# First gather stage of a two-layer graph kernel: attention products moved to a PSUM bank of their own, denominators copied out by ScalarE

## Chip, cores and metric

One core of one Trainium2 chip. The metric is the device time of one execution in microseconds (us), the median of repeated runs. Engines in profile rows: PE (TensorE matmul), PEld (its weight load), DVE (VectorE), ACT (ScalarE), POOL (GpSimd), SP (SyncE, which issues DMAs).

## What is computed

A two-layer graph network on 6,250 nodes of 256 features and 100,000 edges sorted by target. The stage of the change computes, of layer 0, the neighbour sums with the first matmul of the graph block, and the linear attention:

```python
agg = segment_sum(xn[src], dst)                 # 100,000 rows gathered
h1 = (agg + xn) @ W1                            # 1024 columns, batch statistics
q, k = elu(q) + 1, elu(k) + 1                   # of rmsnorm(xn) @ w_qkv
z = 1 / (q . sum(k) + 1e-6)                     # "denominators", per head
h = xn + ((q * z) @ kv) @ w_out + b_out         # "product" is (q * z) @ mix
x0 = x + h + rmsnorm(h)
```

`mix` is kv times w_out, 256x256, made once. Beside this the stage computes the edge network of layer 1 for the first edges (10 to 64 features, Silu, 64 to 1), which the change only has as a neighbour.

## The kernel before, in words

The stage is the phase "g1". Each engine has a queue written out in advance: `timeline` (called at lines 861, 880, 958, 1199, 1397) goes over steps 0 to 737 and, for each work item, emits its parts at fixed numbers of steps ("lags") behind the item's own step. The order on every engine is thus fixed by tables; semaphores (`Steps.wait`) order the engines among themselves. In the lists (`dens`, `zs`, `outs`, `hsum`, ...) `X.wait(e, i, "name")` waits for that part of item i.

- **Gathers** (line 876, POOL): one indirect DMA of 128 rows a step, steps 0 to 701, into 12 pairs of buffers (`got`). Gather 24 later waits for the sums of the pair (`summed`).
- **Sums** (`sums`, line 1261, PE): 8 matmuls per pair of gathers with a one-hot matrix (made by DVE, line 598), ten steps after the pair. DVE adds the result to a ring (`accumulate`, lines 1063 and 1072). The results lie in two PSUM banks; in the pairs of groups behind the edge network (`AFTER`) in four, 0, 1, 2 and 7 (`bank_of`).
- **Up-projection** (`turn_h` 1380, `form_h` 1084, `project_up` 1393, `copy_up` 944, `stats` 1189): 25 batches of 250 nodes. For each PE turns the own rows, DVE adds the ring, PE does 4 x 8 matmuls, ACT copies, DVE takes statistics. Batches come 14 to 22 steps apart, the last one at step 716.
- **Attention** (`ATT`): 50 tiles of 125 nodes, one every 7 steps, the first at step 333. SP loads queries, rows and x (`load_att`, lag 0, behind the last addition of tile i-4). PE: denominators (`denominators`, 1328, lag 8). DVE: `divide` (lag 10) copies them out of PSUM with 1e-6 added (1136), inverts (1138), multiplies with the queries (1140). PE: product (`product`, 1335, lag 13). DVE: `add_h` (1150, lag 15). Then ACT square, root, gate (915, 923, 929), and DVE `finish` (1159, 1161, lag 29). Lag 15 of tile i-1 and lag 8 of tile i are the same step.
- **Edge network** (`EDGE`, steps 391 to 451, its parts up to step 464): hidden layer on PE into bank 7 (1362), Silu on ACT (956), multiply and reduce on DVE (1175, 1178).

Denominators and product of a tile use different columns of PSUM bank 3, and every user of the bank takes turns:

```python
def denominators(i):                       # PE, lag 8
    a_in.wait(e, i % AR, i // AR)
    hsum.wait(e, i - 1, "h")               # add_h of the tile before, DVE
def divide(i):                             # DVE, lag 10
    dens.wait(e, i, "den")
    outs.wait(e, i - 1, "out")
```

Of the kernel before, what the change touches and what calls it, by code (L numbers as in the profile page):

```python
# [26 lines left out]
ALU = mybir.AluOpType  # L27
ACT = mybir.ActivationFunctionType
# [3 lines left out]
N, D, E = 6250, 256, 100000  # L32
# [104 lines left out]
def gps_kernel(nc, A, out):  # L137
# [55 lines left out]
    with top:  # L193
# [431 lines left out]
        with Phase("g1") as ph:  # L625
# [55 lines left out]
            gw = ph.sb("gw", [TN, D])  # L681
            eps = ph.sb("eps", [TN, 1])

# [52 lines left out]
            dens = ph.steps("dens", "den")  # L736
            zs = ph.steps("zs", "eps", "inv", "qz")
            outs = ph.steps("outs", "out")
# [42 lines left out]
            def bank_of(q):  # L781
                return (0, 1, 2, 7)[q % 4] if q in AFTER else q % 2

# [5 lines left out]
            with nc.Block() as block:  # L789
                @block.sync  # L790
                def _(e):
# [66 lines left out]
                    def load_edges(i):  # L858
                        rcopy.wait(e, ST - 1, "T")
                        load_chunk(e, emb, 0, e_in)  # L860
                    timeline(LAST_STEP, ([u - 10 for u in UPS], [(load_own, 0)]), ([WTS[-1] + 8], [(load_edges, 0)]),
                             (QKV, [(load_xn, 0), (store_q, 23)]), (ATT, [(store_att, 32), (load_att, 0)]),
                             (UPS[:-2], [(store_h, 16)]), ([QKV[0] + 34], [(load_rest, 0)]))
# [19 lines left out]
                def _(e):  # L883
# [20 lines left out]
                    def acts_q(i):  # L904
# [4 lines left out]
                        acts.done(e.activation(rq[:, :, :], bank, ACT.Relu), "rq")  # L909

                    def square(i):
                        hsum.wait(e, i, "h")
                        sqs.wait(e, i - 1, "sq")
                        roots.wait(e, i - AR, "root")
                        sqs.done(e.activation(sq[:, :], hh[:, i % AR, :], ACT.Square,
                                              accum_out=ss[:, i % AR:i % AR + 1]), "sq")

                    def root(i):
                        sqs.wait(e, i, "sq")
                        inverse.wait(e, i - AR, "inv")  # L920
                        if i == 0:
                            e.wait_ge(s_eps, 1)
                        roots.done(e.activation(rr[:, i % AR:i % AR + 1], ss[:, i % AR:i % AR + 1], ACT.Sqrt,
                                                bias=eps[:, 0:1], scale=1.0 / D), "root")

# [27 lines left out]
                    def do_silu(i):  # L953
# [6 lines left out]
                             (QKV, [(acts_q, 20), (acts_kv(1), 17), (acts_kv(0), 15), (copy_xr, 10)]),  # L960
                             (ATT, [(one_plus, 26), (root, 20), (square, 17)]),
                             *((UPQ[q], [(copy_up(q), 2)]) for q in (3, 2, 1, 0)))
# [4 lines left out]
                def _(e):  # L967
# [164 lines left out]
                    def divide(i):  # L1132
                        dens.wait(e, i, "den")
                        outs.wait(e, i - 1, "out")
                        bank = ps[:, 3, 0:2 * TN].rearrange("p (c n) -> p c n", c=DC)
                        zs.done(e.tensor_scalar(den[:, :, :], bank, 1e-6, None, ALU.add), "eps")
                        zs.wait(e, i, "eps")
                        zs.done(e.reciprocal(den[:, :, :], den[:, :, :]), "inv")
                        zs.wait(e, i, "inv")
                        zs.done(e.tensor_tensor(qz[:, :, :], qt[:, i % AR, :, :], den[:, :, :], ALU.mult), "qz")  # L1140
# [5 lines left out]
                    def add_h(i):  # L1146
                        xp_out.wait(e, i % AR, i // AR - 1)
                        outs.wait(e, i, "out")
                        hsum.wait(e, i, "xb")
                        hsum.done(e.tensor_tensor(hh[:, i % AR, :], xa[:, i % AR, :], ps[0:TN, 3, 250:250 + D], ALU.add), "h")  # L1150

# [41 lines left out]
                    def aggregate(q):  # L1193
                        def stage(_):
                            stat.wait(e, NB - 1, str(q))
                            for c in (2 * q, 2 * q + 1):
# [8 lines left out]
                             (MIX, [(mix_copy, 3), (mix_turned, 1), (mix_parts, 0)]),  # L1205
                             (ATT, [(finish, 29), (invert, 23), (add_h, 15), (divide, 10), (add_xb, 8)]),
                             *((UPQ[q], [(stats(q), 4)]) for q in (3, 2, 1, 0)),
# [19 lines left out]
                def _(e):  # L1227
# [20 lines left out]
                    def sums(g):  # L1248
# [4 lines left out]
                        if g // 2 in AFTER and bank_of(g // 2) == 2:  # L1253
                            scaled.wait(e, 0, "wr")
                        if g // 2 in AFTER and bank_of(g // 2) == 7:
                            silu.wait(e, NV - 1, "silu")
                        r = copies(w)
# [64 lines left out]
                    def denominators(i):  # L1322
                        a_in.wait(e, i % AR, i // AR)
                        hsum.wait(e, i - 1, "h")
                        if i == 0:
# [6 lines left out]
                    def product(i):  # L1332
                        zs.wait(e, i, "qz")
                        for c in range(DC):
                            mm = e.matmul(ps[0:TN, 3, 250:250 + D], qz[:, c, :], mix[:, c, :],
                                          start=(c == 0), stop=(c == DC - 1))
                        outs.done(mm, "out")
# [46 lines left out]
                    def project_up(q):  # L1384
                        def stage(i):
# [4 lines left out]
                            for k in range(2):  # L1390
                                f = (2 * q + k) * P
                                for c in range(DC):
# [8 lines left out]
                                    (sum_heavy, 7)]),  # L1401
                             (MIX, [(mix_out, 3), (mix_turn, 1)]), (ATT, [(product, 13), (denominators, 8)]),
                             *((UPQ[q], [(project_up(q), 0)]) for q in (3, 2, 1, 0)), (UPS, [(turn_h, 0)]),
# [1652 lines left out]
```

How the kernel before makes its waits and increments, by code:

```python
    def wait(self, eng, i, name):  # L82
        value = i * len(self.names) + self.names.index(name) + 1
        if not isinstance(value, int) or value > 0:
            eng.wait_ge(self.sem, value)
# [16 lines left out]
    def wait(self, eng, u, h):  # L103
        value = 16 * self.per * (h + 1)
        if not isinstance(value, int) or value > 0:
            eng.wait_ge(self.sems[u], value)
# [142 lines left out]
            @block.gpsimd  # L249
            def _(e):
                e.memset(ident[:, :], 0.0).then_inc(s_const, 1)
                e.iota(iota[:, :], pattern=[[1, P]], base=0, channel_multiplier=0,
                       allow_small_or_imprecise_dtypes=True).then_inc(s_const, 1)
                e.memset(ones[:, :], 1.0).then_inc(s_const, 1)
                e.memset(neg_half[:, :], -0.5).then_inc(s_const, 1)
                e.wait_ge(s_const, 1)
                e.affine_select(out=ident[:, :], in_=ident[:, :], compare_op=ALU.not_equal, fill=1.0, base=0,
                                pattern=[[-1, P]], channel_multiplier=1).then_inc(s_const, 1)
                e.wait_ge(s_const, 5)
# [1 line left out]
        def chained(e, ins, s, box):  # L261
            box[0] += 1
            ins.then_inc(s, 1)
            e.wait_ge(s, box[0])
# [67 lines left out]
                @block.sync  # L333
# [5 lines left out]
                    for k, name in enumerate(("src", "dst")):  # L339
                        e.dma_start(raw_i[0:full, k, :], A[name][0:full * RU].rearrange("(r u) -> r u", u=RU)).then_inc(s_in, 16)
                    e.wait_ge(s_fill, 2)
                    for k, name in enumerate(("src", "dst")):
```

## Time and profile before

| | us |
|---|---|
| median of 3 runs (3142.08 to 3146.80) | 3145.21 |
| the profiled execution | 3143.74 |
| its span in the trace | 3142.1 |
| busy in the span: PE, POOL, DVE, ACT | 2647.7, 1809.6, 1739.7, 1429.4 |
| attention of the stage: first denominators, last add | 495.4, 967.8 |
| last matmul of the stage ends | 996.2 |

Times in rows are counted from the start of the span. A row of waits names who waited, for whom, the sum, the number of times and the longest; "issue" is time in front of an instruction for which the profile shows no other engine. A row of the timeline has start and duration, and in brackets how long its engine stood idle before it, and for what.

### The profile page before, as it was taken

Reading aid. Unit: us, or ns where it says so; the run is one execution under the profiler, and the core shown is the slowest. Engines: PE = TensorE matmul, PEld = TensorE weight load, DVE = VectorE, ACT = ScalarE, POOL = GpSimd, SP = SyncE. Lnnn points to the kernel's source line nnn. Section 1 sums busy time; section 2 is a strip of 40 time slices with the busy share of each in tenths; the row PEclk is TensorE's granted clock in tenths of the full one; section 3 lists DMA queues with packets and bytes.
Section 4 is the critical chain, followed back from the end, with each engine's and each line's share of the span. In section 5 each row is a group of like instructions: output and inputs, shape, how many; then the busy total and the mean of one; then the engine's idle time right before and its main releaser. Section 6 shows DMA issues by size and latency. Waiting matters only on the chain. (4 is left out here: it accounts for less than half of the span.)

```text
span 3142.1 us, 54187 instructions
## 1 busy us (share of the span) xinstructions
PE 2647.7 (84%) x14909; PEld 2219.0 (71%) x14909; DVE 1739.7 (55%) x5390; ACT 1429.4 (45%) x3996; POOL 1809.6 (58%) x1962
## 2 busy tenths in 40 slices
PE   1999998898988998699933899999887888689998
PEld 1877778777887886688832666666676677578886
DVE  7733336787776567333355556566566667533333
ACT  4022222442222553233346988788566766322221
POOL 5777777767773355344476777777777777200000
PEclk9999999999999998899965999999999999899999
DMA  7364446667673774333367444444466655422222
GB/s 224 113 190 144 136 140 200 222 198 219 216 220 123 215 237 146 103 95 95 92 186 233 116 125 117 125 117 128 121 181 177 176 162 161 123 76 72 70 65 55
DMA packets 291700, 464.77 MB, mean 148 GB/s; under 512 B 91221, under 2 KB 224276, under 8 KB 290074
## 3 DMA queue, kind: packets, MB, share of 16 engines
q1 hardware_dynamic: 207804, 232.37, 25.2%
q0 software_dynamic: 81216, 221.98, 24.0%
q10 hardware_dynamic: 2402, 7.19, 0.7%
q8 instruction: 115, 1.88, 0.2%
q14 instruction: 163, 1.34, 0.1%
HBM read 349.16 MB, written 112.23 MB: 147 GB/s over the span
## 5 line engine op out<-in xcount | busy, mean ns | idle before, releaser
L2484 POOL DMA_INDIRECT g_got<-xm_d,idx x782 | 757.4, 969 | 253.6 <-issue 219.4
L876 POOL DMA_INDIRECT g_got<-xn_d,idx x702 | 680.4, 969 | 240.5 <-issue 211.3
L2131 PEld LDWEIGHTS ps<-g_hotw,g_got 128*128 128x128 f32 x3128 | 402.3, 196 | 161.6 <-issue 81.3
L2131 PE MATMUL ps<-g_hotw,g_got 128*128 128x128 f32 (+11 forms) x3128 | 423.0, 285 | 91.0 <-DMA g_got<-xm_d,idx 59.9
L1261 PEld LDWEIGHTS ps<-g_hot,g_got 128*128 128x128 f32 x2808 | 357.5, 196 | 80.4 <-DMA g_got<-xn_d,idx 37.7
L1261 PE MATMUL ps<-g_hot,g_got 128*128 128x120 f32 (+4 forms) x2808 | 372.2, 280 | 36.4 <-DMA g_got<-xn_d,idx 25.7
L2533 ACT ACTIVATE g_hotw<-g_hot,g_wr 128x16 f32<-128x16 f32 (+8 forms) x1308 | 300.8, 309 | 90.8 <-DVE g_hot L598 90.2
L1453 POOL TENSOR_TENSOR p_ln_rs<-p_ln_pre,neg_half 125x2 f32<-125x2 f32 x50 | 35.2, 704 | 518.2 <-DVE p_ln_pre L1448 518.2
L2614 DVE TENSOR_TENSOR g_ring<-g_ring,ps 128x84 f32 (+10 forms) x391 | 133.4, 341 | 305.9 <-PE ps L2131 155.8
L2047 POOL DMA_INDIRECT z_d<-p_yj,p_to x108 | 121.9, 1128 | 205.1 <-DVE p_to L2080 183.3
L2934 ACT ACTIVATE p_hid<-ps,p_b 128x250 f32<-128x250 f32 x200 | 82.9, 466 | 278.6 <-PE ps L2896 278.6
L2011 PE MATMUL ps<-gin_hid,p_wj 128*128 128x256 f32 x864 | 197.4, 382 | 1.1 <-ACT gin_hid L1953 0.8
L1662 PE MATMUL ps<-gin_w,gin_hid 128*125 128x256 f32 x800 | 190.4, 388 | 9.1 <-POOL p_before L1721 9.1
L2913 PE MATMUL ps<-p_w,p_hid 128*125 128x256 f32 x800 | 179.2, 382 | 22.2 <-ACT p_hid L2934 22.2
L1393 PE MATMUL ps<-g_hT,g_w 128*128 128x250 f32 x800 | 191.9, 384 | 0.8 <-DVE g_hT L1084 0.8
L1072 DVE TENSOR_TENSOR g_ring<-g_ring,ps 128x40 f32 (+9 forms) x351 | 74.0, 211 | 208.7 <-PE ps L1261 125.7
L2896 PE MATMUL ps<-p_f3T,p_w 128*128 128x250 f32 x800 | 175.3, 375 | 13.3 <-DMA p_w<-in_L_ffn_W 13.3
L2913 PEld LDWEIGHTS ps<-p_w,p_hid 128*125 128x125 f32 x800 | 148.2, 188 | 52.9 <-ACT p_hid L2934 30.2
L2737 PE MATMUL ps<-g_half 128*125 128x512 f32 x400 | 184.9, 605 | 0.0
L2011 PEld LDWEIGHTS ps<-gin_hid,p_wj 128*128 128x128 f32 x864 | 165.1, 191 | 24.4 <-issue 1.1
L1962 ACT ACTIVATE gin_hid<-ps,p_wj 128x256 f32<-128x256 f32 x216 | 90.7, 471 | 188.6 <-PE ps L2011 188.6
L2896 PEld LDWEIGHTS ps<-p_f3T,p_w 128*128 128x128 f32 x800 | 151.6, 190 | 33.1 <-issue 13.4
(376 smaller groups left out, 5042.3 us busy)
## 6 DMA issues: line engine op xcount, KB each, us to landing
h_d<-gin_hid SPq DMA_DIRECT2D x23, 1000.0 KB, 7.8
gin_hid<-h_d SPq DMA_DIRECT2D x23, 1000.0 KB
p_xr<-jobs_d SPq DMA_DIRECT2D x54, 258.0 KB, 2.9
g_got<-xm_d,idx POOLq DMA_INDIRECT x782
g_half<-xmT_d SPq DMA_DIRECT2D x100, 125.0 KB
g_got<-xn_d,idx POOLq DMA_INDIRECT x702
p_wj<-z_d SPq DMA_DIRECT2D x50, 224.0 KB
q_d<-g_qo SPq DMA_DIRECT2D x25, 250.0 KB
```

Source lines behind the costliest of these rows:

```text
L876: landed.start(e.indirect_dma_start(got[:, k % (2 * GB), :], None, xn_d[0:N, :], bass.IndirectOffsetOnAxis(ap=idx[:, HT + k:HT + k + 1], a ...
L1261: mm = e.matmul(to, got[:, 2 * (g % GB) + j, c * P:(c + 1) * P], hot[:, g % HR, j, 0:w].unsqueeze(1).broadcast_to([P, r, w]), start=(j == ...
L1393: mm = e.matmul(ps[:, 5 + n % 2, k * BN:(k + 1) * BN], w1[:, c, f:f + P], hT[:, i % 2, c, :], start=(c == 0), stop=(c == DC - 1))
L1662: mm = e.matmul(ps[0:TN, i % 2, t * D:(t + 1) * D], hid[:, slot(i), c, t * TN:(t + 1) * TN], w2[:, c, :], start=(c == 0), stop=(c == HC - 1))
L2011: mm = e.matmul(ps[:, 2 * k + u, o * JOB:(o + 1) * JOB], w[:, c, o * P:(o + 1) * P], src[:, u, c, :], start=(c == 0), stop=(c == DC - 1))
L2131: mm = e.matmul(to, rows[j][:, c * P:(c + 1) * P], hotw[:, j, c * w:4 * w].unsqueeze(1).broadcast_to([P, r, n]), start=(j == 0), stop=(j = ...
L2484: landed.start(e.indirect_dma_start(got[:, 2 * (g % GB) + j, :], None, xm_d[0:N, :], bass.IndirectOffsetOnAxis(ap=idx[:, 2 * g + j:2 * g + ...
L2533: ins = e.activation(hotw[:, u, 1, m * w:(m + 1) * w], hot[:, u, 1, 0:w], ACT.Copy, scale=chunk(n)[:, k, m:m + 1])
L2614: added.done(e.tensor_tensor(to, to, sums_of(bank_of(g)[0], w, bank_of(g)[1]), ALU.add), "add")
L2737: mm = e.matmul(ps[0:TN, bank, :], kT[:, i % 2, c, :], wkv[:, c, at:at + INNER], start=(c == 0), stop=(c == DC - 1))
L2896: mm = e.matmul(ps[:, q, m * BN:(m + 1) * BN], w1[:, k, c, f * P:(f + 1) * P], f3T[:, u, :, c * TN:(c + 1) * TN], start=(c == 0), stop=(c ...
L2913: mm = e.matmul(ps[0:TN, 4 + u, t * D:(t + 1) * D], hid[:, u, k, f, t * TN:(t + 1) * TN], w2[:, k, f, :], start=(j == 0), stop=(j == 2 * F ...
```

## The change

Tiles whose product falls behind the edge network (`ALONE` = 18 and later) put the product into bank 7, columns 0 to 255, in place of bank 3; the sums of `AFTER` then rotate through banks 0, 1 and 2. `ATT` is split into `NEAR` (tiles 0 to 17) and `FAR` (18 to 49). For all tiles, ACT copies the denominators out of PSUM with 1e-6 added (`move_den`, a new activation Identity with bias `eps`, lag 9 or 10), and DVE's `divide` begins with the reciprocal, in place, behind that copy (`moved`). From tile 19 on the denominators no longer wait for `add_h` of the tile before, only for `moved`; the product waits for that `add_h`. In `FAR` everything behind the denominators, the product included, stands one step later.

```diff
@@ -679,7 +679,7 @@
-            eps = ph.sb("eps", [TN, 1])
+            eps = ph.sb("eps", [P, 1])
@@ -734,7 +734,8 @@
             dens = ph.steps("dens", "den")
-            zs = ph.steps("zs", "eps", "inv", "qz")
+            moved = ph.steps("moved", "den")
+            zs = ph.steps("zs", "inv", "qz")
             outs = ph.steps("outs", "out")
@@ -779,7 +780,16 @@
             def bank_of(q):
-                return (0, 1, 2, 7)[q % 4] if q in AFTER else q % 2
+                return q % 3 if q in AFTER else q % 2
+
+            ALONE = next(i for i, at in enumerate(ATT) if at + 14 > EDGE[-1] + 15)
+            NEAR, FAR = ATT[:ALONE], ATT[ALONE:]
+
+            def far(stage):
+                return lambda i: stage(ALONE + i)
+
+            def out_at(i):
+                return (7, 0) if i >= ALONE else (3, 250)
@@ -859,7 +869,7 @@
                     timeline(LAST_STEP, ([u - 10 for u in UPS], [(load_own, 0)]), ([WTS[-1] + 8], [(load_edges, 0)]),
-                             (QKV, [(load_xn, 0), (store_q, 23)]), (ATT, [(store_att, 32), (load_att, 0)]),
+                             (QKV, [(load_xn, 0), (store_q, 23)]), (ATT, [(store_att, 33), (load_att, 0)]),
                              (UPS[:-2], [(store_h, 16)]), ([QKV[0] + 34], [(load_rest, 0)]))
@@ -908,6 +918,16 @@
+                    def move_den(i):
+                        dens.wait(e, i, "den")
+                        zs.wait(e, i - 1, "qz")
+                        if i == 0:
+                            e.wait_ge(s_eps, 1)
+                        if i <= ALONE:
+                            outs.wait(e, i - 1, "out")
+                        moved.done(e.activation(den[:, :, :], ps[:, 3, 0:2 * TN].rearrange("p (c n) -> p c n", c=DC),
+                                                ACT.Identity, bias=eps[:, 0:1]), "den")
+
                     def square(i):
@@ -921,7 +941,7 @@
                         roots.done(e.activation(rr[:, i % AR:i % AR + 1], ss[:, i % AR:i % AR + 1], ACT.Sqrt,
-                                                bias=eps[:, 0:1], scale=1.0 / D), "root")
+                                                bias=eps[0:TN, 0:1], scale=1.0 / D), "root")
@@ -958,7 +978,8 @@
                              (QKV, [(acts_q, 20), (acts_kv(1), 17), (acts_kv(0), 15), (copy_xr, 10)]),
-                             (ATT, [(one_plus, 26), (root, 20), (square, 17)]),
+                             (NEAR, [(one_plus, 26), (root, 20), (square, 17), (move_den, 9)]),
+                             (FAR, [(far(one_plus), 27), (far(root), 21), (far(square), 18), (far(move_den), 10)]),
                              *((UPQ[q], [(copy_up(q), 2)]) for q in (3, 2, 1, 0)))
@@ -1130,11 +1151,8 @@
                     def divide(i):
-                        dens.wait(e, i, "den")
+                        moved.wait(e, i, "den")
                         outs.wait(e, i - 1, "out")
-                        bank = ps[:, 3, 0:2 * TN].rearrange("p (c n) -> p c n", c=DC)
-                        zs.done(e.tensor_scalar(den[:, :, :], bank, 1e-6, None, ALU.add), "eps")
-                        zs.wait(e, i, "eps")
                         zs.done(e.reciprocal(den[:, :, :], den[:, :, :]), "inv")
@@ -1147,7 +1165,8 @@
                         hsum.wait(e, i, "xb")
-                        hsum.done(e.tensor_tensor(hh[:, i % AR, :], xa[:, i % AR, :], ps[0:TN, 3, 250:250 + D], ALU.add), "h")
+                        bank, at = out_at(i)
+                        hsum.done(e.tensor_tensor(hh[:, i % AR, :], xa[:, i % AR, :], ps[0:TN, bank, at:at + D], ALU.add), "h")
@@ -1203,7 +1222,8 @@
                              (MIX, [(mix_copy, 3), (mix_turned, 1), (mix_parts, 0)]),
-                             (ATT, [(finish, 29), (invert, 23), (add_h, 15), (divide, 10), (add_xb, 8)]),
+                             (NEAR, [(finish, 29), (invert, 23), (add_h, 15), (divide, 10), (add_xb, 8)]),
+                             (FAR, [(far(finish), 30), (far(invert), 24), (far(add_h), 16), (far(divide), 11), (far(add_xb), 9)]),
                              *((UPQ[q], [(stats(q), 4)]) for q in (3, 2, 1, 0)),
@@ -1252,8 +1272,6 @@
                             scaled.wait(e, 0, "wr")
-                        if g // 2 in AFTER and bank_of(g // 2) == 7:
-                            silu.wait(e, NV - 1, "silu")
                         r = copies(w)
@@ -1321,7 +1339,9 @@
                         a_in.wait(e, i % AR, i // AR)
-                        hsum.wait(e, i - 1, "h")
+                        moved.wait(e, i - 1, "den")
+                        if i <= ALONE:
+                            hsum.wait(e, i - 1, "h")
                         if i == 0:
@@ -1331,8 +1351,13 @@
                         zs.wait(e, i, "qz")
+                        if i == ALONE:
+                            silu.wait(e, NV - 1, "silu")
+                        if i > ALONE:
+                            hsum.wait(e, i - 1, "h")
+                        bank, at = out_at(i)
                         for c in range(DC):
-                            mm = e.matmul(ps[0:TN, 3, 250:250 + D], qz[:, c, :], mix[:, c, :],
+                            mm = e.matmul(ps[0:TN, bank, at:at + D], qz[:, c, :], mix[:, c, :],
                                           start=(c == 0), stop=(c == DC - 1))
@@ -1399,7 +1424,8 @@
                                     (sum_heavy, 7)]),
-                             (MIX, [(mix_out, 3), (mix_turn, 1)]), (ATT, [(product, 13), (denominators, 8)]),
+                             (MIX, [(mix_out, 3), (mix_turn, 1)]), (NEAR, [(product, 13), (denominators, 8)]),
+                             (FAR, [(far(product), 14), (far(denominators), 8)]),
                              *((UPQ[q], [(project_up(q), 0)]) for q in (3, 2, 1, 0)), (UPS, [(turn_h, 0)]),
```

Two places of the new order, each first of the kernel before and then of the changed one. PE between the products of tile 35 and the denominators of tile 36 (`g1_qz` are the divided queries, `g1_qt` the queries, `g1_a0` their loads, `g1_hsum` the semaphore of `add_h`, `g1_moved` that of ACT's copy), before:

```order
L1335 MATMUL ps<-g1_mix,g1_qz 125x256 [waits g1_zs]
L1335 MATMUL ps<-g1_mix,g1_qz 125x256
L1393 MATMUL ps<-g1_hT,g1_w1 128x250 [waits g1_upcopy,g1_formed]
L1393 MATMUL ps<-g1_hT,g1_w1 128x250 x3
L1261 MATMUL ps<-g1_hot,g1_got 128x120 [waits g1_added,g1_ready,g1_got3]
L1261 MATMUL ps<-g1_hot,g1_got 128x120 x3
L1328 MATMUL ps<-g1_qt,g1_ksd 128x125 [waits g1_hsum,g1_a0]
L1328 MATMUL ps<-g1_qt,g1_ksd 128x125
L1393 MATMUL ps<-g1_hT,g1_w1 128x250 [waits g1_upcopy,g1_formed]
```

changed (lines 1360 product, 1418 up-projection, 1279 sums, 1348 denominators):

```order
L1418 MATMUL ps<-g1_hT,g1_w1 128x250 [waits g1_upcopy,g1_formed]
L1418 MATMUL ps<-g1_hT,g1_w1 128x250 x3
L1360 MATMUL ps<-g1_mix,g1_qz 125x256 [waits g1_hsum,g1_zs]
L1360 MATMUL ps<-g1_mix,g1_qz 125x256
L1279 MATMUL ps<-g1_hot,g1_got 128x120 [waits g1_added,g1_ready,g1_got3]
L1279 MATMUL ps<-g1_hot,g1_got 128x120 x3
L1348 MATMUL ps<-g1_qt,g1_ksd 128x125 [waits g1_moved,g1_a0]
L1348 MATMUL ps<-g1_qt,g1_ksd 128x125
L1418 MATMUL ps<-g1_hT,g1_w1 128x250 [waits g1_upcopy,g1_formed]
```

The product stands behind the block of the up-projection that it stood in front of, and waits for `g1_hsum` too; the denominators wait for `g1_moved` where they waited for `g1_hsum`.

DVE from `add_h` of tile 35 to the multiplication of the queries of tile 36 (`g1_ring` the ring, `g1_hst` the statistics), before:

```order
L1150 TENSOR_TENSOR g1_hh<-g1_xa,ps 125x256 [waits g1_hsum,g1_outs,g1_xp3]
L1144 TENSOR_TENSOR g1_xa<-g1_xa,g1_bout 125x256 [waits g1_a0]
L598 TENSOR_TENSOR g1_hot<-iota,rel_all 128x2x40 [waits g1_summed]
L1155 RECIPROCAL g1_rr<-g1_rr 125x1 [waits g1_gate,g1_roots]
L1136 TENSOR_SCALAR g1_den<-ps 128x250 [waits g1_outs,g1_dens]
L1138 RECIPROCAL g1_den<-g1_den 128x250 [waits g1_zs]
L1140 TENSOR_TENSOR g1_qz<-g1_qt,g1_den 128x250 [waits g1_zs]
```

changed (lines 1169 `add_h`, 1156 reciprocal, 1158 multiplication):

```order
L1169 TENSOR_TENSOR g1_hh<-g1_xa,ps 125x256 [waits g1_hsum,g1_outs,g1_xp3]
L1162 TENSOR_TENSOR g1_xa<-g1_xa,g1_bout 125x256 [waits g1_a0]
L1174 RECIPROCAL g1_rr<-g1_rr 125x1 [waits g1_gate,g1_roots]
L1208 BN_STATS g1_hst<-gin_hid 128x6 [waits g1_upcopy]
L1208 BN_STATS g1_hst<-gin_hid 128x6
L1084 TENSOR_LOAD base_i
L1084 ISA x2
L1093 ISA [waits g1_joined,g1_added,g1_summed]
L1093 TENSOR_TENSOR g1_ring<-g1_ring,ps 128x2x40
L598 TENSOR_TENSOR g1_hot<-iota,rel_all 128x2x40 [waits g1_summed]
L1156 RECIPROCAL g1_den<-g1_den 128x250 [waits g1_outs,g1_moved]
L1158 TENSOR_TENSOR g1_qz<-g1_qt,g1_den 128x250 [waits g1_zs]
```

The instruction of line 1136 is gone, the reciprocal (1138, now 1156) waits for `g1_moved`, and statistics and one ring add now stand between `add_h` of one tile and the reciprocal of the next.

## Rows read from the trace of the kernel before

**Rows 1.** Windows: us busy (x instructions) of PE, PEld, DVE, ACT, POOL
```profile
540.00:692.00 152.00, 137.83 (x842) 117.90 (x840) 119.75 (x320) 72.91 (x151) 110.49 (x114) 1.00 0.69 218
692.00:985.00 293.00, 257.19 (x1671) 239.50 (x1672) 213.90 (x610) 71.64 (x190) 207.29 (x217) 0.96 0.67 211
```

**Rows 2.** Gathers, 692 to 985 us: ns min/median/max, first, last start
```profile
L876 POOL DMA_INDIRECT g_got<-xn_d,idx x217: 942/947/1306, 691.3 to 966.1; - x109
```

**Rows 3.** Waits of POOL, 640 to 692: us, times, longest
```profile
POOL g_got L876 <- PE ps L1261: 8.6, 7, 1.9
```

**Rows 4.** Waits of POOL, 692 to 967 us
```profile
POOL g_got L876 <- issue: 57.8, 189, 0.4
POOL g_got L876 <- PE ps L1261: 10.3, 28, 2.0
```

**Rows 5.** Windows of line 1261, the sums: PE, PEld busy (x)
```profile
480.00:1000.00 520.00, 200.55 (x1528) 194.55 (x1528) 0.97 0.65 204
692.00:1000.00 308.00, 123.63 (x952) 122.46 (x952) 0.96 0.64 201
967.00:1000.00 33.00, 9.45 (x78) 9.38 (x77) 1.00 0.20 66
```

**Rows 6.** Windows of line 876, the gathers: POOL busy (x)
```profile
480.00:1000.00 520.00, 363.18 (x378) 0.97 0.65 204
692.00:1000.00 308.00, 207.29 (x217) 0.96 0.64 201
```

**Rows 7.** Waits of PE, 692 to 985 us
```profile
PE ps L1328 <- DVE g_hh L1150: 29.8, 13, 4.2
PE ps L1335 <- DVE g_qz L1140: 5.6, 6, 1.6
```

**Rows 8.** Waits of PE, 540 to 692 us
```profile
PE ps L1328 <- DVE g_hh L1150: 4.9, 5, 1.4
PE ps L1261 <- DVE g_ring L1072: 0.9, 2, 0.5
```

**Rows 9.** Timeline, tiles 35 and 36: start, us, engine, line
```profile
840.55 0.41 DVE L1150 TENSOR_TENSOR g_hh<-g_xa,ps 125x256 f32<-125x256 f32 x1
...
841.68 0.61 PE L1328 MATMUL ps<-g_qt,g_ksd 128*128 128x125 f32 x4
...
842.34 0.42 DVE L1136 TENSOR_SCALAR g_den<-ps 128x250 f32<-128x250 f32 x1 [0.74 <-PE ps L1328]
...
842.79 1.72 DVE L1138 RECIPROCAL g_den<-g_den 128x250 f32<-128x250 f32 x1
...
844.54 0.42 DVE L1140 TENSOR_TENSOR g_qz<-g_qt,g_den 128x250 f32<-128x250 f32 x1
...
848.43 0.42 DVE L1150 TENSOR_TENSOR g_hh<-g_xa,ps 125x256 f32<-125x256 f32 x1
```

**Rows 10.** Timeline of PE at the end of the stage
```profile
980.04 1.91 PE L1261 MATMUL ps<-g_hot,g_got 128*128 128x88 f32 x16
...
983.52 1.02 PE L1261 MATMUL ps<-g_hot,g_got 128*128 128x88 f32 x8
...
989.15 7.04 PE L1393 MATMUL ps<-g_hT,g_w 128*128 128x250 f32 x32 [0.77 <-DVE g_hT L1084]
```

**Rows 11.** An activation of the copy's shape, in a later stage
```profile
L1636 ACT ACTIVATE p_rh<-ps,p_rb 128x250 f32<-128x250 f32 x25 | 11.5, 459 | 4.8 <-PE ps L1684 4.6
```

**Rows 12.** Timeline of ACT between Silu and Sqrt
```profile
610.39 0.60 ACT L956 ACTIVATE g_attr<-ps 128x512 f32<-128x512 f32 x1 [3.46 <-DVE g_attr L1175]
...
611.04 0.59 ACT L929 ACTIVATE g_gw<-g_wn,ones,g_rr 125x256 f32<-125x256 f32 x1
...
611.53 0.58 ACT L944 ACTIVATE gin_hid<-ps 128x500 f32<-128x500 f32 x1
...
612.13 1.28 ACT L923 ACT_TABLE_LOAD   x1
```

**Rows 13.** Waits of DVE, 692 to 985 us
```profile
DVE g_ring L1072 <- issue: 37.4, 57, 2.0
```

## The prediction, made before the changed kernel ran

> **What bounds the kernel now.** I looked for the stage first. The change touches only the first gather stage, whose last matmul ends at 996.2 of 3142.1 us; nothing behind it is edited, so what this stage gives or takes goes one to one into the total. The busy table by stretches [rows 1] has two parts that matter: 540 to 692 us (edge network, attention and up-projection together) and 692 to 985 us (no edge network). PE is the busiest engine in both (137.8 of 152 us, 257.2 of 293 us).
>
> The pace is set elsewhere. GpSimd issues one gather after another: in the second stretch 217 of them, started from 691.3 to 966.1 [rows 2]. Each takes 0.947 us (median) and has 57.8 / 189 = 0.31 us in front of it [rows 4]: 1.25 us. One step of the schedule holds one gather, so a step can't be shorter than 1.25 us. GpSimd was held back by PE for 8.6 us in 7 waits before 692 us [rows 3] and 10.3 us in 28 waits after it [rows 4]; each wait contains the 0.3 us that every gather has in front of it anyway, so the real losses are 8.6 - 2.1 = 6.5 us and 10.3 - 8.4 = 1.9 us.
>
> How late is PE? The sums take 8 matmuls for 2 gathers, so matmuls still to come, divided by 4, less gathers still to come, is PE's backlog in gathers. At 480 us: 1528/4 - 378 = 4. At 692 us: 952/4 - 217 = 21 [rows 5, 6]. At 967 us, all gathers issued: 78/4 = 19.5 [rows 5]. There are buffers for 24. So PE falls behind while the edge network runs, stays near the edge of the buffers, and pays for it in the tail: the last gather ends at 966.1 + 0.9 = 967.0 [rows 2], the last sums group starts at 983.5, and PE ends at 996.2 [rows 10].
>
> Why doesn't it catch up after 692? It waits 29.8 us in 13 waits at line 1328, the denominators, for VectorE's add at line 1150, and 5.6 us at line 1335 for the divided queries [rows 7]. One pass shows the ring [rows 9]: the add of tile 35 ends at 840.96, the denominators of tile 36 run 841.68 to 842.29, VectorE copies (0.42), inverts (1.72) and multiplies (0.42) until 844.96, and adds PE's product at 848.43; only then may the denominators of tile 37 start. Denominators and product share bank 3, so each engine waits for the other, and the add and the next denominators stand in the same step.
>
> **The change part by part.**
> *The ring is cut* from tile 19 on (31 passes; tile 18 still waits). The denominators then wait only for Scalar's copy of the tile before, five steps old; the product waits for an add that is five steps old. The 29.8 us go, if nothing takes their place. Next in line are the quotient (due at step +11, used at +14, as before three steps) and the tile's loads, issued at VectorE's step +2, used at +8: six steps of 1.25 us, where it had seven.
>
> *What this is worth.* PE can't get ahead of the gathers. At 480 us it ran 4 behind. With 4 left, two groups and an up block stand between the last gather and the last group: 980.04 to 983.52, 3.5 us [rows 10]. So the last group starts near 967.0 + 3.5 = 970.5 in place of 983.5: **-13.0 us**. The rest of PE's work to 996.2 is the same work in the same order. For that PE must win 13.0 us plus the 1.9 us by which GpSimd gets earlier, 14.9 of the 29.8 us. Half of what goes may come back elsewhere for nothing.
>
> *GpSimd's waits behind 692 us* go: **-1.9 us**.
>
> *Tiles 0 to 18 (to 692 us).* VectorE loses one instruction of 0.42 us and its 0.03 us of spacing per pass; Scalar gets one, 128x250 from PSUM, whose nearest row is 0.459 us [rows 11]. Where VectorE is late, it gains 0.44; where it waits for the denominators, the path from their end to the reciprocal goes from 842.79 - 842.29 = 0.50 us [rows 9] to some 0.05 + 0.46 + 0.05 = 0.56. Ends: 19 passes by +0.06 each, +1.1 us; and everything GpSimd lost there, -6.5 us. PE waits only 4.9 us for the add [rows 8] in that stretch, and is 91% busy, so little can be won: I take **-1.5 us**, nearer the upper end. The Trainium skill (VectorE: DVE Perf Modes, the TRN2 errata) would price Scalar's instruction at (172 + 250) cycles of 1.2 GHz, 0.35 us; this trace says 0.459 for the shape, and I go by the trace. By the page the sum would be better by at most 19 x 0.11 = 2 us.
>
> *Scalar's order.* The copy stands between other activations. It has room: 72.9 of 152 us busy [rows 1]. Identity after Silu comes without a table load (610.39, then 611.04; the load is in front of the root at 612.13) [rows 12], so no loads are added. Behind it wait the up-projection's copies, by at most 0.46 us; PE needs those several steps later: nothing.
>
> *VectorE.* 213.9 us busy and 37.4 us of register work in front of the ring adds [rows 1, 13] in 293 us, less 31 x 0.45 = 14 us: 237 us, 81%. It won't bound.
>
> *Sums in three banks instead of four.* A group then waits for the add of the group pair three earlier. Before 692 us there are two banks, and PE waited 0.9 us for ring adds in 152 us [rows 8]. Bounds: 0 and 293/152 x 0.9 = 1.7 us; three banks are nearer 0, and a wait there would only use up slack: nothing. GpSimd, SP and all other queues issue the same instructions; stores and the last additions come a step later and aren't the tail (the last addition is at step 706, PE's last matmul at 723).
>
> Sum: -13.0 - 1.9 - 1.5 = **-16.4 us**. The profiled execution took 3143.74 us (span 3142.1 and 1.6 around it), the median of the runs is 3145.21, 1.5 higher; from that, 3145.2 - 16.4 = **3128.8 us**. What a measurement of this kernel can tell from no change is about 0.2%, 6.3 us.
>
> **The rivals.**
> *A. The wait moves.* PE stops at the product for the quotient, or at the denominators for the loads. For: the quotient takes 2.6 us, and between up-projections PE reaches the product at once (5.6 us in 6 waits already [rows 7]). Against: VectorE is no longer stopped either, and half may come back free. If each of 31 passes paid 0.8 us, 25 of 29.8 us would be back: -4.8 - 1.5, about 3139; half as bad, 3132.
>
> *B. Scalar holds the quotient back in the edge network's stretch: slower.* Its queue is in order; a table load, a Silu and an up-projection copy in front are 1.28 + 0.60 + 0.58 = 2.46 us [rows 12]. Some 10 passes fall there: 24.6 us more on a ring that is still closed, and GpSimd stands at once, since the buffers are nearly full. Less the 14.9 us of the later part: +9.7, about 3155. It decides from 14.9 + 6.3 = 21.2 us, 2.1 us per pass. Against: Scalar is busy for half of the stretch [rows 1], and in the timeline its instruction ahead of the place of the copy has ended before the denominators in each of these passes.
>
> *C. Four banks were needed.* The Trainium skill (Perfetto Trace Analysis, Matmuls) asks to rotate independent groups through different banks so that evacuation overlaps. The change rotates the sums less. From tile 19 on there are some 60 pairs of groups; 29.8 / 60 = 0.5 us of waiting for an add on each would give back all that the ring gave: no change, 3144. The 0.9 us over 152 us with only two banks [rows 8] speak against it. That page's rule also favours the product's own bank.
>
> **How the numbers follow.** Forecast case 0.70 (3120 to 3134: from 3145.2 - 16.5 - 1.9 - 6.5, the last group starting with the end of the last gather, to a PE that keeps 8 gathers of backlog, -9.5 - 1.9, and wins nothing early). A 0.18, two thirds of it over 0.2% faster. C, or a change that for another reason does nothing, 0.06. B 0.06. Faster: 0.70 + 0.12 = 0.82; same 0.06 + 0.06 = 0.12; slower 0.06. The range reaches from 3120, everything won, into A's worse half, 3140. PE's clock was 0.96 in the second stretch [rows 1], half speed for some 8% of it; a stretch more or less in the tail moves the end by 1.7 us, inside the range.
>
> **What would show it.** Right: PE's wait at the denominators for the add is gone after tile 19; matmuls left at the last gather fall from 78 to about 16 to 24; GpSimd doesn't wait for PE after 700 us; PE's last matmul of the stage comes 15 to 17 us earlier; PE now waits for gathered rows. Wrong: a new wait of over 15 us at the product or for the tile's loads (A), more GpSimd waits before 692 us (B), PE waiting for ring adds (C).

## The result, and the profile of the changed kernel

| | before | changed |
|---|---|---|
| median of the runs, 4 and 4, us | 3145.74 (3142.08 to 3146.8) | 3123.32 (3122.14 to 3128.59) |
| profiled execution, us; span | 3143.74; 3142.1 | 3123.76; 3122.2 |
| mean granted clock of TensorE | 0.942 | 0.943 |
| last matmul of the first gather stage ends, us | 996.2 | 979.8 |

The changed kernel takes 0.9939 of the time, 95% interval 0.9926 to 0.9951, which is 15 to 23 us of the time before; the two medians lie 22.4 us apart. The forecast was 16.4 us, 3128.8, in a range of 3120 to 3140.

Busy time by stretches, in the columns of [rows 1]:

```profile
540.00:692.00 152.00, 140.51 (x868) 121.07 (x867) 117.28 (x315) 80.18 (x171) 115.82 (x119) 1.00 0.70 224
692.00:985.00 293.00, 262.23 (x1692) 240.51 (x1691) 208.64 (x595) 85.16 (x221) 205.23 (x214) 0.97 0.66 208
```

PE runs more matmuls in the same time in both stretches, and GpSimd issued five more gathers from 540 to 692 us (119 for 114). The gathers after 692 (columns of [rows 2]), and GpSimd's waits from 640 to 692 and from 692 to 967 us ([rows 3, 4] before):

```profile
L886 POOL DMA_INDIRECT g_got<-xn_d,idx x214: 942/949/1204, 691.4 to 961.2; - x107
```
```profile
POOL g_got L886 <- PE ps L1279: 1.1, 3, 0.5
...
POOL g_got L886 <- issue: 57.9, 190, 0.3
POOL g_got L886 <- PE ps L1279: 7.3, 24, 0.3
```

No wait after 692 is longer than the 0.3 us that every gather has in front of it: GpSimd no longer loses anything there. The last gather starts at 961.2, 4.9 us earlier than in [rows 2] (2.3 us earlier in a second profile of the changed kernel, below).

The sums (first three rows) and the gathers (last two), counted as in [rows 5, 6]:

```profile
480.00:1000.00 520.00, 196.96 (x1528) 190.92 (x1528) 0.97 0.66 207
692.00:1000.00 308.00, 118.97 (x936) 117.67 (x935) 0.96 0.64 201
962.00:1000.00 38.00, 3.05 (x26) 2.99 (x24) 0.87 0.19 55
...
480.00:1000.00 520.00, 366.42 (x380) 0.97 0.66 207
692.00:1000.00 308.00, 205.23 (x214) 0.96 0.64 201
```

PE's backlog is 1528/4 - 380 = 2 gathers at 480 us (4 before), 936/4 - 214 = 20 at 692 (21 before), and 26/4 = 6.5 at 962 us, where the last gather ends (19.5 at 967 us before). It still falls behind under the edge network; now it catches up behind it. What it waits for, 692 to 985 us and then 540 to 692 us ([rows 7, 8] before; the third number is the longest wait):

```profile
PE ps L1348 <- DMA g_x<-in_x: 14.7, 12, 2.3
PE ps L1360 <- DVE g_qz L1158: 5.9, 9, 1.2
PE ps L1418 <- DVE g_hT L1105: 4.6, 3, 3.0
...
PE ps L1348 <- DVE g_hh L1169: 5.4, 5, 1.4
PE ps L1279 <- DVE g_hot L598: 5.1, 4, 1.9
PE ps L1279 <- DVE g_ring L1093: 0.7, 2, 0.5
```

The 29.8 us for the add at the denominators (line 1348, was 1328) are gone. Half of them came back as waits for the tile's loads, 14.7 us. The quotient costs 5.9 us (5.6 before), and from 692 us on no wait for a ring add shows with three banks for the sums. PE's largest wait from 540 to 692 us in the kernel before, which [rows 8] leaves out, is that for the one-hot matrix of the sums, which VectorE makes:

```profile
PE ps L1261 <- DVE g_hot L598: 7.6, 3, 3.0
```

It is 5.1 us in the changed kernel. The tail, as in [rows 10]:

```profile
963.68 1.91 PE L1279 MATMUL ps<-g_hot,g_got 128*128 128x88 f32 x16
...
967.15 1.02 PE L1279 MATMUL ps<-g_hot,g_got 128*128 128x88 f32 x8
...
972.79 7.04 PE L1418 MATMUL ps<-g_hT,g_w 128*128 128x250 f32 x32 [0.77 <-DVE g_hT L1105]
```

The last sums group starts at 967.15 for 983.52: 5.0 us behind the end of the last gather (961.2 + 0.95), for 16.5 before. The stage ends 16.4 us earlier, at 979.83. This is the number forecast, but of other parts: -4.9 for the gathers (forecast -3.4), -11.5 for the tail (forecast -13.0). That the two errors cancel to the tenth is luck: the second profile of the changed kernel has -2.3, -12.5 and together -14.8.

**The other 3.5 us of the span** (19.9 in all) come where the program is the same, in the next stage. The difference between the two profiles is -17.3 us at 1185 us of before and -20.7 at 1245. PE before, then PE changed, at the same place of the program:

```profile
1197.69 1.33 PE L1684 MATMUL ps<-p_f1T,p_rw 128*128 128x250 f32 x4 [1.89 <-ACT p_f1T L1627]
1198.82 3.40 PE L1662 MATMUL ps<-gin_w,gin_hid 128*125 128x256 f32 x8
```
```profile
1178.57 1.11 PE L1710 MATMUL ps<-p_f1T,p_rw 128*128 128x250 f32 x4
1179.52 1.89 PE L1688 MATMUL ps<-gin_w,gin_hid 128*125 128x256 f32 x8
```

Before, Scalar had stood 6.73 us for a load of hidden rows (4.69 in the changed kernel), PE then stood 1.89 us, and its next eight matmuls took 3.40 us for 1.89, with a granted clock of 0.50 from 1199 to 1201 us, the lower of its two levels (1.2 GHz); the changed kernel's is 1.00 at the same place. In all 13 other profiles of this case the same eight matmuls take 1.89 us, one of the kernel before on another chip among them (below). So it belongs to that one profile of before, and not to the change. It therefore doesn't explain the time either, which is a median of runs: of the 15 to 23 us, the profiles account for 16.4, and whether the rest is more than scatter stays open.

### The profile page after: what moved, and what is told of

The parts are those of the page before. It is cut to its first block and busy times, and to the rows that moved or that the text cites. A ratio compares the mean times of both kernels' runs of the same rounds, so it can differ in the third digit from the quotient of the medians.

```text
span 3122.2 us, 54248 instructions
## 1 busy us (share of the span) xinstructions
PE 2645.5 (85%) x14909; PEld 2211.8 (71%) x14909; DVE 1716.8 (55%) x5340; ACT 1446.5 (46%) x4046; POOL 1819.7 (58%) x1962
```

## The experiments

Twelve runs of nine kernels in three batches. The first and the third met other chips (the record calls them 0 and 4), on which every version has a median of 3548 to 3586 us; the second met one like that of the result (14 in the record). The diffs are shortened to the lines that matter. The theory from the profile: the copy on Scalar brings the gathers forward in the edge network's stretch, the product's own bank brings the tail forward, and they add up. Its rivals: one part does all of it; or the bank's release is what counts and the loads now cap it, so that more is to be had there.

### First batch: the parts, on a slower chip

Copy on Scalar alone (for all tiles; all in bank 3 as before, sums in four banks):
```diff
-  zs.done(e.tensor_scalar(den, bank, 1e-6, None, ALU.add), "eps")   # VectorE, divide(i)
+  moved.done(e.activation(den, bank, ACT.Identity, bias=eps), "den")  # ScalarE, move_den(i)
```


> The kernel before with ScalarE's copy of the denominators alone (for all 50 tiles at lag 9); the product stays in bank 3, the sums in four banks, the ring of denominators, quotient, product and add is closed. Theory 1 (two gains that add up: the copy relieves VectorE while the edge network runs, which takes GpSimd's waits before 692 us away, and the cut ring shortens PE's tail): about 5 us under the kernel before, 3140 to 3142; last gather near 961, PE's wait at the denominators still 25 us or more after 692 us. Theory 2 (the 0.45 us less on VectorE in 50 passes is the whole gain): 3124 to 3130. Theory 3 (only the cut ring counts): 3145, and longer waits at the denominators.

Banks alone (the changed kernel with the copy back on VectorE):
```diff
-  moved.wait(e, i, "den")            # divide(i)
+  dens.wait(e, i, "den")
+  zs.done(e.tensor_scalar(den, bank, 1e-6, None, ALU.add), "eps")
   ...
-  moved.wait(e, i - 1, "den")        # denominators(i)
+  zs.wait(e, i - 1, "eps")
```


> The changed kernel with VectorE's own copy of the denominators back, and no copy on ScalarE; product in bank 7 from tile 18 on, sums in three banks, denominators wait for VectorE's copy of the tile before. Theory 1: the tail's part alone and GpSimd's losses before 692 us as in the kernel before: 12 to 16 us under the kernel before, 3130 to 3134; last gather near 964 to 966. Theory 2: 3140 or more. Theory 3: as the changed kernel, 3123.

Three banks for the sums alone (the kernel before otherwise):
```diff
-  return (0, 1, 2, 7)[q % 4] if q in AFTER else q % 2
+  return q % 3 if q in AFTER else q % 2
```


> The kernel before with the sums behind the edge network in banks 0, 1 and 2 in place of 0, 1, 2 and 7, and nothing else. If three banks are enough: within 2 us of the kernel before, and PE's waits for ring adds after 692 us under 1 us. If the fourth bank was worth something, and the changed kernel only covers it: 5 us or more slower, with waits of PE for ring adds.

The changed kernel with earlier loads, for all tiles:
```diff
-  fin.wait(e, i - AR, "y")
+  hsum.wait(e, i - AR, "h")      # queries and attention input
   ...
+  fin.wait(e, i - AR, "y")       # only the copy of x, with a landing of its own
```


> The changed kernel, but a tile's queries and rows are loaded as soon as the add of four tiles before is done, and only its x waits for the last addition; the denominators no longer wait for x. The new wait of PE in the changed kernel (14.7 us in 12 waits at the denominators, for loads) should be gone. Theory 1, the gathers set the pace: PE's backlog falls faster, last gather unchanged within 1 us, last sums group 1 to 2 us earlier: 3121 to 3123. Rival, PE sets the pace, so that each microsecond it doesn't wait counts: 3109 to 3112.

Measured, against 3582.47 us (35 runs) of the kernel before on this chip:

| | median us | ratio | interval |
|---|---|---|---|
| copy alone | 3582.1 | 0.9999 | 0.9980 to 1.0017 |
| banks alone | 3580.4 | 1.0000 | 0.9980 to 1.0020 |
| three banks alone | 3585.93 | 1.0008 | 0.9987 to 1.0029 |
| changed, early loads | 3576.54 | 0.9992 | 0.9973 to 1.0010 |

Nothing can be told from no change here. **Three banks alone** fits its first case, that three banks are enough: its time can't be told from that of the kernel before, and from 820 to 1175 us, behind the edge network, PE has no wait for a ring add, as in the kernel before on chip 4. What differs from the result's chip shows in GpSimd's waits over all its gathers. The kernel before was not profiled on this chip, so these rows are its own from the third batch's; the four versions above have 98.7 to 117.4 us of "remote" in 45 to 49 waits and 106.3 to 150.1 us for PE. The chip of the result has 211.3 us of "issue", 29.2 of PE and nothing else:

```profile
POOL g_got L876 <- issue: 205.0, 576, 17.7
POOL g_got L876 <- PE ps L1261: 139.7, 81, 8.4
POOL g_got L876 <- remote: 90.9, 45, 3.1
```
```profile
855.72 0.99 POOL L876 DMA_INDIRECT g_got<-xn_d,idx  x1 [0.30 <-issue]
857.01 0.95 POOL L876 DMA_INDIRECT g_got<-xn_d,idx  x1 [0.30 <-issue]
860.54 0.94 POOL L876 DMA_INDIRECT g_got<-xn_d,idx  x1 [2.58 <-remote]
```

GpSimd stands 45 times, 2.0 us on average, from 2 to 66 gathers apart, and the trace names none of the program's own semaphores or queues for it. PE is far behind the gathers by the 300th of them (the sums start 25.9 us after their gather's end, 22.4 to 26.7 in the four versions above, where the result's chip has 4.0), so that the buffers are full and GpSimd waits for PE from then on. The prediction's premise, that the gathers set the pace and PE catches up in the tail, doesn't hold on these chips. Whether the changed kernel gains there as a whole was not timed.

### Second batch: the same, on a chip like that of the result

> The changed kernel once more, as it is. The first four experiments met a chip on which the kernel before takes 3582 us in place of 3145, and GpSimd stands for 2 to 3 us after every ten to twelve gathers. If this run meets a chip like the first one: ratio 0.993 to 0.995, last gather 4 to 5 us earlier than in the kernel before and the stage's last matmul 15 to 18 us earlier. If it meets a chip like the second: theory 1 (the gain is PE being held back by the ring while the gathers run on time) says the ratio is 0.998 or more, since there the gathers themselves come late; a rival, that the ring costs 0.6% wherever it runs, says 0.994 there too.

> ScalarE's copy alone, as in e1_copy_alone. On a chip like the first: theory 1 (two gains that add up) 3140 to 3142, last gather near 961, PE still waits 25 us or more at the denominators after 692 us; theory 2 (VectorE's 0.45 us in 50 passes is the whole gain) 3124 to 3130; theory 3 (only the cut ring counts) 3145.

> The banks alone, as in e2_banks_alone. On a chip like the first: theory 1 3130 to 3134, last gather 964 to 966; theory 2 3140 or more; theory 3 3123.

> The changed kernel with the loads of queries and rows earlier, as in e4_early_loads. On a chip like the first: the 14.7 us of PE's waits for loads gone; theory 1 (the gathers set the pace) 3121 to 3123, last gather unchanged within 1 us; rival (PE sets the pace) 3109 to 3112.

The same kernels under new names, against 3153.64 us of the kernel before (17 runs, 3142.09 to 3159.33):

| | median us | ratio | interval | last gather starts | last group starts | PE ends |
|---|---|---|---|---|---|---|
| before (first profile) | | | | 966.1 | 983.5 | 996.2 |
| changed (first profile) | | | | 961.2 | 967.2 | 979.8 |
| changed, again | 3126.88 | 0.9924 | 0.9906 to 0.9943 | 963.7 | 968.8 | 981.4 |
| copy alone | 3138.96 | 0.9961 | 0.9945 to 0.9977 | 961.0 | 977.4 | 990.1 |
| banks alone | 3129.78 | 0.9937 | 0.9921 to 0.9953 | 967.3 | 977.6 | 990.3 |
| changed, early loads | 3132.97 | 0.9942 | 0.9927 to 0.9957 | 971.0 | 976.2 | 988.8 |

The last three columns are single profiles; two of the same kernel differ by 2.5 us at the last gather, and the kernel before was not profiled in this batch. **Copy alone**: the gathers end as early as with the whole change, and the tail is nearly as long as before, 15.5 us for 16.5. **Banks alone**: the gathers end as late as before, the tail is 9.3 us. **Both**: 4 to 5 us of tail. The waits show why. Copy alone, 692 to 985 us, and its tail:

```profile
PE ps L1335 <- DVE g_hh L1157: 28.9, 14, 3.9
PE ps L1342 <- DVE g_qz L1147: 3.6, 4, 1.3
```
```profile
977.44 1.02 PE L1268 MATMUL ps<-g_hot,g_got 128*128 128x88 f32 x8
```

The ring of 29.8 us is whole, 28.9: the copy on Scalar doesn't touch it. Banks alone, PE in the same stretch, and GpSimd from 640 to 967 us:

```profile
PE ps L1352 <- DVE g_qz L1150: 13.7, 10, 2.6
PE ps L1340 <- DMA g_x<-in_x: 13.0, 16, 1.5
PE ps L1410 <- DVE g_hT L1094: 3.5, 5, 1.2
```
```profile
POOL g_got L885 <- PE ps L1271: 16.4, 34, 2.1
```

The ring is gone, but PE now stops at the product for the quotient, 13.7 us for 5.9 and 6.4 in the two profiles with the copy on Scalar. This is rival A's mechanism, and the copy holds it down: VectorE has one instruction less between the denominators and the quotient. By the ends of the stage, the copy gives 6.1 us, the banks 5.9 and both 14.8 or 16.4, so that 3 to 4 us would come only from both together.

The times don't bear this out, and don't exclude it. By their ratios the copy alone gives 7 to 17 us, the banks alone 15 to 25 and both 18 to 30: each part alone is clearly faster than the kernel before, and both together are faster than the copy alone. The whole change and the banks alone can't be told apart, and taken at the middle of their intervals the parts add up to 32 us, more than the whole's 24. The stage doesn't hold all of it. From the stage's end to the end of the span, where the program is the same in all, the profiles take 2145.9 us (before), 2142.4 and 2141.4 (changed), 2142.2 (copy), 2137.8 (banks) and 2135.0 (early loads). This scatter is as large as the shares, and what makes it stays open.

Of the expectations, these were missed: the copy alone was to give 3 to 5 us and the banks alone 12 to 16, both less than measured; the last gather of the changed kernel was to come 4 to 5 us earlier and came 2.3 earlier, and that of the banks alone was to start by 966 and started at 967.3. The changed kernel's ratio (0.993 to 0.995 expected) and stage end (15 to 18 us earlier expected, 14.8 measured) lie at the edge.

What the copy does in the edge network's stretch, 540 to 692 us, with 0.3 us taken off each of GpSimd's waits for PE: with it GpSimd loses 0.3, 2.5 (the change) and 1.3 us (copy alone), without it 6.5 (before) and 6.1 us (banks alone). PE's wait for the one-hot matrix is 5.1, 5.2 and 5.9 us with it, 7.6 and 6.6 without. From the 440th to the 485th gather the gaps between PE's matmuls sum to 8.4 us before, 5.2 with the copy alone, 4.0 and 4.6 in the two profiles of the change, and 5.9 with the banks alone. The last number lies so near the others that the gaps alone don't prove the copy's share. GpSimd's waits speak for it, but they are five single profiles, and the early loads below have the copy too and lose 9.4 us. What is shown is that the copy alone is faster (0.9961); that it works through these waits is the reading that fits best.

**Early loads** took the load waits away, as meant, and made nothing faster. Both theories missed: the time isn't below the changed kernel's, where the rival asked for 11 us or more, and the last gather didn't stay but came 7 to 10 us later. Its waits of PE, 692 to 985 us, and of GpSimd, 540 to 692 us (10.4 us in 13 before):

```profile
PE ps L1363 <- DVE g_qz L1160: 10.7, 11, 3.2
PE ps L1282 <- DMA g_got<-xn_d,idx: 7.2, 6, 2.9
PE ps L1421 <- DVE g_hT L1107: 6.5, 6, 2.2
```
```profile
POOL g_got L888 <- PE ps L1282: 14.5, 17, 1.8
```

PE waits for gathered rows in place of loads, and longer for the quotient (10.7 us): behind 692 the gathers are the bound, and the 14.7 us of load waits used slack. The last gather is later (971.0) because of GpSimd's losses before 692; why they grew with loads that start earlier stays open (it is one profile).

### Third batch: sizes, on a slower chip

> The kernel before, unchanged, for a second profile. Its first profile differs from those of the changed kernel and of the parts by another 3 us behind the stage, at 1185 to 1245 us, where the program is the same. If that belongs to the one execution: TensorE's last matmul of the stage at 994 to 998 us, last gather 964 to 968, backlog 16 to 21 gathers at the end, and from the stage's end to the span's end 2 to 4 us less than the first profile's 1145.9 + the rest, as in all the others. If it is something that the change does to the later stages: the same length behind the stage as in the first profile. The time is that of the kernel before by both.

Two banks for the sums (in the changed kernel):
```diff
-  return q % 3 if q in AFTER else q % 2
+  return q % 2
```


> The changed kernel with the sums in two PSUM banks in place of three behind the edge network. My theory, that the number of banks for the sums doesn't bind here: waits of TensorE for ring adds of at most 2 us between 692 and 967 us, last sums group within 1 us of the changed kernel's (967 to 969), time 0 to +2 us against the changed kernel. Rival C carried on, that one bank fewer begins to bind: over 5 us of waits for ring adds, backlog at the last gather above 8 gathers, stage end 2 to 8 us later.

Early loads only behind the edge network (in the changed kernel):
```diff
-  fin.wait(e, i - AR, "y")
+  if i > ALONE:
+      hsum.wait(e, i - AR, "h")
+  else:
+      fin.wait(e, i - AR, "y")
```
`AR` is 4: the wait is for the tile four before, not eight as the text below says. As in the early loads of the first batch, x has a landing of its own, behind the last addition, so that for all tiles the denominators no longer wait for x.


> The changed kernel with the queries' and attention inputs' loads let go at the sum of the tile eight before (and not at its last addition), only for tiles behind the edge network; the tiles before keep their order, unlike in the earlier version for all tiles. If the gathers set the pace: the 14.7 us of load waits go from the denominators, backlog at the last gather still some 3 to 5 gathers, last gather 961 to 964, stage end within 1.5 us of the changed kernel's. If load waits still cost: stage end 2 to 5 us earlier. If earlier loads hurt by themselves (as the last gather at 971.0 with all tiles early could say): last gather above 966.

Half a product (in the changed kernel, from tile 18 on; its result leaves out half of the sum):
```diff
-  for c in range(DC):
+  used = 1 if i >= ALONE else DC
+  for c in range(used):
```


> The changed kernel, the attention product of tiles 19 to 49 over only the first 128 of its 256 rows: one matmul in place of two, so some 13 us less work for TensorE between 692 and 985 us. Leaves out half of that sum. If the gathers set the pace and TensorE keeps up (my theory): last gather where it is (960 to 964), the last sums group at most 1 to 2 us earlier, stage end 0 to 2 us earlier. If TensorE's work still bounds the stretch: stage end 8 to 13 us earlier.

| | median us | ratio | interval | last gather starts | PE ends |
|---|---|---|---|---|---|
| before, again | 3558.17 | 1.0004 | 0.9982 to 1.0026 | 1157.1 | 1188.3 |
| two banks | 3554.71 | 0.9987 | 0.9967 to 1.0007 | 1157.9 | 1189.9 |
| early loads behind the edge network | 3550.46 | 0.9977 | 0.9954 to 0.9999 | 1156.2 | 1186.1 |
| half product | 3548.26 | 0.9970 | 0.9951 to 0.9989 | 1148.3 | 1178.2 |

(3562.84 us of the kernel before, 35 runs.) **Before, again.** Absolute times on this chip don't compare, but how the difference to the first profile changes does: it is +192.9 us at 1185 us of before and +190.0 at 1245. The same kernel without some 3 us: they were one execution's.

**Two banks.** Waits of PE for ring adds, 820 to 1175 us:

```profile
PE ps L1279 <- DVE g_ring L1093: 16.2, 7, 4.7
```

The other two changed versions of this batch, with three banks, and the kernel before, with four, have none of this wait in the same window. So rival C's mechanism exists one bank further down, on a chip where PE is always behind. It costs PE 16 us of waits, and the time (0.9987) can't be told from that of the early loads with three banks (0.9977). On the result's chip two banks weren't tried.

**Early loads behind the edge network** and **half a product** are the only two below 1 by their intervals, by 8 and 11 us, on a chip where PE's lateness holds back GpSimd throughout. Taking some 13 us of work from PE ends its stage 8 to 12 us earlier than in the two versions above, in single profiles: this speaks for PE's work as the bound there. The medians show less of it, 2.2 and 6.5 us. So this run tells nothing of the result's chip, for which it was made; that the gathers are the bound there rests on GpSimd's waits and on the early loads of the second batch. No version was shown to beat the changed kernel, and the changed kernel itself was not timed on the slower chips.

## Why the prediction was right, step by step

- *The ring is cut.* Right: 29.8 us gone, and with the banks alone as well (no row), not with the copy alone (28.9).
- *The tail, -13.0.* Right, a little large: -11.5. The last group starts 5.0 us behind the last gather where I took 3.5, because 6.5 gathers are left, not 4. In the second profile the last group starts 4.0 us behind it, and the tail is -12.5.
- *GpSimd's waits after 692, -1.9.* Right: no loss is left.
- *Tiles 0 to 18, -1.5.* This term was too small for what it was taken from, GpSimd's losses there: 6.5 us became 0.3 and 2.5 in the two profiles, -6.2 and -4.0. At the last gather less arrives, -3.0 and -0.4 (4.9 and 2.3, each less 1.9), since each gather itself took 975 and 976 ns on average for 969, over 702 gathers 4 to 5 us. Why is open; with the banks alone it is 976 too. I had taken a value far from the bound of -6.5, since PE waits only 4.9 us for the add there. PE still waits 5.4 us for the add. The weak step was to price the copy by the one wait that it lies on: the larger wait of 7.6 us, for the one-hot matrix that VectorE makes, isn't in [rows 8], and it is this one that fell.
- *The copy's price, 0.46.* The row of the changed kernel, 500 to 985 us:

```profile
L928 ACT ACTIVATE g_den<-ps,g_eps 128x250 f32<-128x250 f32 x49 | 23.0, 470 | 119.8 <-PE ps L1348 117.3 <-issue 2.5
```

  0.470 us, and no table load is added. There are 20 table loads before 1000 us in both kernels. VectorE waited for the copy 2.6 us in 3 waits after 692, 3.0 us in 5 from 540 to 692. By the Trainium skill (VectorE: DVE Perf Modes, the TRN2 errata) it would be an estimated 0.35 us, (172 + 250) cycles of 1.2 GHz; this trace doesn't agree.
- *Three banks, nothing.* Right on the result's chip: no wait for a ring add after 692. The Trainium skill (Perfetto Trace Analysis, Matmuls) asks to rotate groups through banks; how many are enough, the runs show for this kernel: three, in every profile with three behind the edge network; with two, 16.2 us of waits appear, on a slower chip.
- *Rival A* came in part: 14.7 us of load waits, just under the 15 us that I gave as its sign, and they cost nothing in the end, since they used slack. For the quotient it came with the banks alone (13.7 us) and with the early loads (10.7). *Rival B*: GpSimd's waits before 692 fell. *Rival C*: not with three banks; see two banks.
- *What would show it.* Matmuls left at the end of the last gather: 26, where I gave 16 to 24 (6.5 gathers of backlog). I said that PE would now wait for gathered rows: after 692 it doesn't in the first profile of the changed kernel, does for 2.6 us in 3 waits in the second, and for 7.2 us with early loads. These two say that PE only just caught up.
- *The total.* The stage gave 16.4 and 14.8 us in the two profiles, the times 15 to 23 us at first and 18 to 30 in the second batch. That the stage's number came out to the tenth is luck; that it came from the cut ring and from GpSimd's losses is what the rows show. The sum leaves the stretch behind the stage at nothing; there the profiles scatter by several us, and it is open whether part of the gain lies in it.

## What to carry to other kernels

When two parts of a change each cut a wait on the same path, time them apart: here each was faster alone (ratios 0.9961 and 0.9937), and the rows show how they meet, since the bank's release turns into a wait for the quotient (13.7 us) that the copy then shortens (5.9). Don't split a gain finer than two profiles of the same kernel agree, here 2.5 us. Price a moved instruction by all that waits for its engine, not only by the wait that it lies on. And ask of a wait that appears whether there is slack under it before removing it: 14.7 us of load waits went, and the time didn't fall.

## What was not expected of the hardware

The kernel before takes 3145 and 3154 us on the chips of the result and of the second batch, 3582 and 3563 us on those of the first and third. On chip 4, the third batch's, GpSimd stands 45 times in its 702 gathers (90.9 us), PE and VectorE stand together at the stage's start (until 73, 77, 83 and 89 us, for 3 to 7 us each), and the mean granted clock is 0.897 for 0.942. A gather itself takes the same: 965 ns on average for 969. The cause of these halts stays open. Parts of the change that are worth 0.4 and 0.6% on chip 14 couldn't be told from no change on chip 0.
